# A graph kernel's gathered table: rows 1280 bytes apart in HBM and addressed by element, row slots 1056 bytes apart in SBUF

## What is computed

```
support = x @ W                      # x is normalised first
r_D = sigmoid(support @ a2)
gated = r_D * support
msg = gated[col] * edge_values[:, None]
out = segment_sum(msg, row, num_segments=n)
sumnorm = segment_sum(edge_values * r_D[col, 0], row, num_segments=n)
out = out / sumnorm[:, None]
```

## Time and profile before

| | us |
|---|---|
| median of 3 runs | 1783.61 |
| lowest, highest | 1783.45, 1788.98 |
| the profiled execution | 1787.5 |
| its span, first to last instruction | 1785.2 |
| GpSimd busy with the 599 gathers of L727 | 582.6 |
| GpSimd busy with the 294 gathers of L649 | 296.7 |
| TensorE busy, whole program | 1240.0 |
| VectorE busy, whole program | 1081.3 |

### The profile page before, as it was taken

One profiled execution on the slowest core, in us unless ns is written; L12 is line 12 of the kernel. 1 busy time (PEld: TensorE's weight loads), 2 busy tenths in 40 slices (PEclk: granted clock), 3 DMA queues, 4 the chain that ended last, 5 costly groups with the idle time before them and its releaser, 6 DMA issues.

```text
span 1785.2 us, 20679 instructions
## 1 busy us (share of the span) xinstructions
PE 1240.0 (69%) x5939; PEld 947.5 (53%) x5939; DVE 1081.3 (61%) x2748; ACT 361.8 (20%) x1172; POOL 945.3 (53%) x956
## 2 busy tenths in 40 slices
PE   5488666876776866565676767667676676768898
PEld 3377555755555655333454544445454454545787
DVE  8978896766787673344555555555555565556322
ACT  1255200000000000011222222222222222223233
POOL 0111176666666666566666666666666666664000
PEclk9699876878878778677787787877788787878999
DMA  7011143333333333733333333333333333332022
GB/s 221 8 58 59 35 76 92 94 90 94 101 87 93 95 88 99 110 99 94 91 94 92 100 97 90 100 90 101 91 99 98 91 100 91 99 94 60 28 71 73
DMA packets 120862, 158.14 MB, mean 89 GB/s; under 512 B 57903, under 2 KB 90307, under 8 KB 120764
## 3 DMA queue, kind: packets, MB, share of 16 engines
q0 software_dynamic: 44528, 119.20, 25.4%
q1 hardware_dynamic: 69180, 31.29, 6.9%
q10 hardware_dynamic: 7056, 6.45, 1.1%
HBM read 134.88 MB, written 21.98 MB: 88 GB/s over the span
## 4 chain that ended last, share of the span: by engine, by line
issue 38%; another core or an unknown queue 23%; PE 18%; DVE 9%; ACT 7%; DMA 2%; SPq 1%; DVEq 0%; POOLq 0%; ACTq 0%
PE bank L1499 17%; ACT big L1445 2%; DMA res<-in_x_dram 1%; ACT xT L1432 1%; DVE big L806 1%; ACT pos L1410 1%; DVE S L1131 1%; ACT xn L1423 1%; ACT lg L1436 1%; DVE neg L1169 1%; DVE ag L1142 1%; DMA srec<-sorted_edges_dram 1%; DVE big L846 1%; ACT bc L1405 0%
## 5 line engine op out<-in xcount | busy, mean ns | idle before, releaser
L727 POOL DMA_INDIRECT rows<-gated_rows_dram,ring_i x599 | 582.6, 973 | 324.6 <-issue 171.3
L1499 PE MATMUL bank<-rows,S 128*128 128x257 f32 (+1 forms) x2254 | 602.1, 412 | 66.3 <-issue 26.2
L1499 PEld LDWEIGHTS bank<-rows,S 128*128 128x128 f32 x2254 | 456.5, 210 | 205.0 <-issue 110.7
L649 POOL DMA_INDIRECT rows<-gated_rows_dram,lg x294 | 296.7, 1009 | 159.7 <-issue 82.9
L1499 PE MATMUL bank<-Wxs,xT 128*128 128x512 f32 x196 | 176.7, 1054 | 270.7 <-ACT xT L1432 270.6
L1499 PE MATMUL bank<-big 128*98 128x80 f32 (+2 forms) x1740 | 217.0, 284 | 145.3 <-issue 97.8
L1499 PEld LDWEIGHTS bank<-big 128*98 128x98 f32 (+1 forms) x1740 | 203.5, 201 | 165.8 <-issue 162.6
L1499 PEld LDWEIGHTS bank<-Wxs,xT 128*128 128x128 f32 x196 | 55.7, 314 | 333.7 <-ACT xT L1432 284.4
L1131 DVE TENSOR_SCALAR S<-iota,lof,srec 128x128 f32<-128x128 f32 x637 | 177.2, 358 | 3.5 <-PE bank L1499 3.1
L637 POOL DMA_INDIRECT sorted_edges_dram<-big,idx x52 | 64.9, 1248 | 202.8 <-ACT big L1318 94.3
L1194 DVE SCALAR_TENSOR_TENSOR bc<-bc 128x1 f32<-128x1 f32 x49 | 10.7, 219 | 246.5 <-ACT bc L1303 246.5
(11 more groups left out here) (226 smaller groups left out, 1326.3 us busy)
## 6 DMA issues: line engine op xcount, KB each, us to landing
rows<-gated_rows_dram,ring_i POOLq DMA_INDIRECT x599
gated_rows_dram<-rows SPq DMA_DIRECT2D x49, 128.5 KB, 2.7
overflow_sums_dram<-ovr ACTq DMA_DIRECT2D x49, 128.5 KB
ovr<-overflow_sums_dram SPq DMA_DIRECT2D x49, 128.5 KB
res<-in_x_dram SPq DMA_DIRECT2D x1, 6144.0 KB
out_dram<-S SPq DMA_DIRECT2D x48, 128.0 KB, 1.7
rows<-gated_rows_dram,lg POOLq DMA_INDIRECT x294
sorted_edges_dram<-big SPq DMA_DIRECT2D x2, 514.5 KB, 7.9
```

The source lines that it names most:

```text
L649: pool.indirect_dma_start(rows[:, turn(n), :], None, gtab[:, :], bass.IndirectOffsetOnAxis(ap=ring1[:, n:n + 1], axis=0)).then_inc(s_row[t ...
L727: pool.indirect_dma_start(rows[:, slot(b, u), :], None, gtab[:, :], bass.IndirectOffsetOnAxis(ap=ring_i[:, b // CH % 2, n:n + 1], axis=0)) ...
L1499: return nc.tensor.matmul(o, l, r, start=start, stop=stop, skip_group_check=True)
```

## The change

The table moves to the tensor that held the lists, and the lists move to the tensor that held the table. The table's rows are TW = 320 elements (1280 bytes) apart. The gather is given the whole tensor as a column of single elements, so its index is the source row's number times 320; `decode` makes that product with one more VectorE instruction. The 63 elements between two rows are set to zero by four new DMAs on SP's queue, which stand between the weights and x; GpSimd waits for them before the first gather. The row slots in SBUF are RSTEP = 264 elements (1056 bytes) apart. Lengths that named the lists (LL) are now LS. The branch for very uneven graphs, which this input does not take, is changed in the same way.

```
+TW = 320
+LL = NB * P * TW // 2
+RSTEP = 264
...
+        table = srt
+        table_rows = table.rearrange("(r w) o -> r (w o)", w=TW)
+        edges = gtab.rearrange("n (w o) -> (n w) o", o=1)
...
-        RW = max(SL * GW, 4736)
+        RW = max(SL * RSTEP, 4736)
...
-        rows = rows_t[:, 0:SL * GW].rearrange("p (u w) -> p u w", w=GW)
+        rows = rows_t[:, 0:SL * RSTEP].rearrange("p (u w) -> p u w", w=RSTEP)[:, :, 0:GW]
...
             for d, s in wloads:
                 sp.dma_start(d, s).then_inc(s_w, 16)
+            for lo in range(0, NB, 13):
+                n = min(13, NB - lo)
+                sp.dma_start(table_rows[lo * P:(lo + n) * P, GW:TW].rearrange("(b p) w -> p b w", p=P),
+                             zeros[:, 0:n * (TW - GW)].rearrange("p (b w) -> p b w", w=TW - GW)).then_inc(s_pad, 16)
             sp.dma_start(res[:, 0:LAST, :], x[0:LAST * P, :].rearrange("(b p) f -> p b f", p=P)).then_inc(s_x, 16)
...
-                sp.dma_start(gtab[ds(b * P, P), :], Gt[:, k, :]).then_inc(s_gd[k], 16)
+                sp.dma_start(table_rows[ds(b * P, P), 0:GW], Gt[:, k, :]).then_inc(s_gd[k], 16)
...
-                        rows[:, turn(n), :], None, gtab[:, :],
+                        rows[:, turn(n), :], None, table[:, :],
                         bass.IndirectOffsetOnAxis(ap=ring1[:, n:n + 1], axis=0)).then_inc(s_row[turn(n)], 16)
...
+            pool.wait_ge(s_pad, 16 * -(-NB // 13))
...
-            v.tensor_scalar(ring, r, 7, None, ALU.logical_shift_right).then_inc(s_idx, 1)
+            step(v.tensor_scalar(ring, r, 7, None, ALU.logical_shift_right))
+            v.tensor_scalar(ring, ring, TW, None, ALU.mult).then_inc(s_idx, 1)
```

More of the change, by code:

```diff
@@ L49 @@
 OFF = NB * PB1
-LL = OFF + NB * PB + OV * P + (EC - ECOL) * P
+LS = OFF + NB * PB + OV * P + (EC - ECOL) * P
 SL = 18
@@ L149, in build @@
         tmpi = carve(EC, I32)
-        zeros = carve(LL // P)
+        zeros = carve(LS // P)
         cnt, ntf, ctf, base = carve(NB), carve(NB), carve(NB), carve(NB)
@@ L307, in build @@
         s_const = sem("s_const")
+        s_pad = sem("s_pad")
         s_tick = sem("s_tick")
@@ L637, in send @@
                 pool.indirect_dma_start(
-                    srt[:, :], bass.IndirectOffsetOnAxis(ap=idx[:, k, h:h + 1], axis=0),
+                    edges[:, :], bass.IndirectOffsetOnAxis(ap=idx[:, k, h:h + 1], axis=0),
                     runs[k][:, h * RUN:(h + 1) * RUN], None).then_inc(s_run, 16)
@@ L682, in scatter @@
                         pool.sem_inc(s_tick, 1)
-                        pool.tensor_scalar(ring_s[:, k, :], ring_s[:, k, :], LL, None, ALU.add)
+                        pool.tensor_scalar(ring_s[:, k, :], ring_s[:, k, :], LS, None, ALU.add)
                     else:
@@ L713, in _ @@
                     pool.indirect_dma_start(
-                        orow, None, gtab[:, :], bass.IndirectOffsetOnAxis(ap=oidx, axis=0)).then_inc(s_orow, 16)
+                        orow, None, table[:, :], bass.IndirectOffsetOnAxis(ap=oidx, axis=0)).then_inc(s_orow, 16)
             pool.wait_ge(s_ovd, 1)
@@ L727, in tile @@
                     pool.indirect_dma_start(
-                        rows[:, slot(b, u), :], None, gtab[:, :],
+                        rows[:, slot(b, u), :], None, table[:, :],
                         bass.IndirectOffsetOnAxis(ap=ring_i[:, b // CH % 2, n:n + 1], axis=0)).then_inc(sem, 16)
@@ L773, in _ @@
             step(v.tensor_scalar(over[0:VB, :], iotap[0:VB, :], float(NB), None, ALU.is_ge))
-            step(v.scalar_tensor_tensor(firstc[0:VB, :], over[0:VB, :], float(LL - NB * PB1), firstc[0:VB, :], ALU.mult, ALU.add))
-            step(v.scalar_tensor_tensor(firstd[0:VB, :], over[0:VB, :], float(LL - NB * PB), firstd[0:VB, :], ALU.mult, ALU.add))
+            step(v.scalar_tensor_tensor(firstc[0:VB, :], over[0:VB, :], float(LS - NB * PB1), firstc[0:VB, :], ALU.mult, ALU.add))
+            step(v.scalar_tensor_tensor(firstd[0:VB, :], over[0:VB, :], float(LS - NB * PB), firstd[0:VB, :], ALU.mult, ALU.add))
             v.tensor_copy(idx[:, 0, 0:1], firstc[0:VB, :]).then_inc(s_idx0, 1)
@@ L1105, in _ @@
                     v.tensor_copy(oreci, orec[:, 0:1]).then_inc(s_oS, 1)
-                    dve.wait_ge(s_oS, t * 4 + 1)
-                    v.tensor_scalar(oidx, oreci, 7, None, ALU.logical_shift_right).then_inc(s_oidx, 1)
+                    dve.wait_ge(s_oS, t * 5 + 1)
+                    v.tensor_scalar(oidx, oreci, 7, None, ALU.logical_shift_right).then_inc(s_oS, 1)
+                    dve.wait_ge(s_oS, t * 5 + 2)
+                    v.tensor_scalar(oidx, oidx, TW, None, ALU.mult).then_inc(s_oidx, 1)
                     v.tensor_scalar(olo[:, 0:1], oreci, P - 1, None, ALU.bitwise_and).then_inc(s_oS, 1)
-                    dve.wait_ge(s_oS, t * 4 + 2)
+                    dve.wait_ge(s_oS, t * 5 + 3)
                     v.tensor_copy(olof, olo[:, 0:1]).then_inc(s_oS, 1)
-                    dve.wait_ge(s_oS, t * 4 + 3)
+                    dve.wait_ge(s_oS, t * 5 + 4)
                     v.tensor_scalar(oS, iota[:, :], olof, orec[:, 1:2], ALU.is_equal, ALU.mult).then_inc(s_oS, 1)
@@ L1658, in _ @@
                     pe.wait_ge(s_orow, t * 16 + 16)
-                    pe.wait_ge(s_oS, t * 4 + 4)
+                    pe.wait_ge(s_oS, t * 5 + 5)
                     pe.wait_ge(s_oadd, t + 1)
```

12 lines of the change are left out of this document (6 added, 6 removed).

## The result

The changed kernel took 1802.76 us (median; 1796.52 to 1804.84). The kernel before, measured beside it, took 1786.3 us. The ratio on record is 1.0078, with a 95% interval of 1.0049 to 1.0106 (the quotient of the two medians is 1.0092): slower by 9 to 19 us. The forecast was 1790.2, in a range from 1775 to 1806, with 0.59 on slower. So the direction was right and the time lies in the range, but 12.6 us over the point. The profiled execution is the quickest of the four (1796.52; span 1793.0 after 1785.2).

The account below looks back on a forecast made before the run. It took the DMA engines loading x to bound the opening and GpSimd's queue the gathering parts. Terms 8.0 + 0.6 + 0 - 2.0 = +6.6 us on the median of 1783.6 gave 1790.2 us, range 1775 to 1806.

Parts of the forecast that it names:

- The bound of the opening: Opening: the 16 DMA engines moving x set the limit; a later x delays VectorE's statistics and everything after equally.
- The pad stores: Opening, SP's queue ahead of x: four stores of 6272 runs add 8.0 us, range 5.8 to 11.6, all on the path.
- The higher bound of 29.7 ns: Opening: the price of one 252-byte run using the dearer fixed cost of 20.3 ns, giving 11.6 us for 392 runs.
- The index: Decodes on VectorE: one more product each, three of 15 before a waiting gather, adding 0.6 us.
- GpSimd's issue: Gathering parts: indexing by element adds 0 us to issuing a gather; the other end was 58 us.
- the dearer issue: Rival, gathering parts: 16 to 65 ns more per gather by element, 1804 to 1848 us; chance 0.10.
- The flight: Gathering parts: aligned rows and slots shorten a gather's transfer, given back at 63 GpSimd stops; gain 2 us.
- GpSimd's queue leads: Gathering parts: GpSimd's queue sets the pace, 1.25 us a gather and a stop of 3 us, 18.0 us a block.
- The rest: Table-row stores, moved lists, GpSimd's wait for the gap-filling stores, and TensorE's reads: no effect on time.
- Dear pads: Rival, opening: the gap-filling stores cost twice their bytes, 15.6 us in place of 8.0, 1798 us; chance 0.12.
- The stops: Rival, gathering parts: GpSimd's waits on the full slot ring, 181 us, vanish with alignment, about 1610 us; chance 0.04.
- the shorter flight: Rival, gathering parts: alignment halves a gather's payload time, saving 16 us over 63 stops, 1776 us; chance 0.10.

Follow-up runs that it names:

- the pads alone: The kernel before plus only the four pad stores ahead of x, into a tensor nothing reads, with GpSimd's wait for them: ratio 1.0052, 9.2 us.
- the pads of 64 columns: The changed kernel with gap-filling stores of columns 256 to 319 (256 bytes from 1024) in place of 63 columns, table stores waiting for them: ratio 1.0033, 5.9 us.
- element index alone: The changed kernel with rows and slots 257 elements apart, so no gap-filling stores and no alignment; gathers still indexed by single elements: ratio 1.0008.
- the table of run prices: Two versions of the kernel before, each with five separately waited store batches of 6272 runs ahead of x, 128 to 512 bytes: 14.7 to 45.7 ns a run.
- the half-row kernel: The changed kernel with each gather fetching only the first 128 of a row's 257 columns, slots filled with ones: ratio 1.0097 against the kernel before.
- wider table stores: The changed kernel without the gap-filling stores; the 49 table-row stores write all 1280 bytes of a row: ratio 0.9989 on one chip, 1.0025 on another.
- the changed kernel's second trace: The changed kernel run again unaltered: ratio 1.0067 against the kernel before, span 1800.1 us.

## Why the prediction was right or wrong

**The bound of the opening: right.** x's load is on the path without slack; what stood ahead of it moved the statistics and the first gather by 11 us, and the end by 9 to 14 (9.2 with the pads alone, 12.0 and 13.9 with the change).

**The pad stores, 8.0 us, bounds 5.8 to 11.6: the place right, the size too small.** They cost 11.0 (50.23 less 39.26), near the upper end. The term of the sum that was mis-sized is the price of a run, 22.0 ns, put together from loads: x's 1024-byte runs and the 24-byte runs of the lists. A run on 32-byte steps is cheaper than that (16.9 ns alone, 15 in place: 6.0 us / 392). These, which begin at 1028, cost 25.0 ns alone and 28 in place (11.0 us / 392). And I took 8.0 where my own price gave 8.6. The higher bound of 29.7 ns would have been the better choice, though for another reason than the one I had for it. My sentence that SP's four issues run in some 0.43 us each while the engines work off the weights was wrong as well: they took 8.55 us, though that time is not what they cost (above, the pads of 64 columns).

**The index, 0.6 us: not contradicted.** With the statistics 10.97 later, the first gather is 11.24 later. The 0.27 between them has the size of the first decode's product, but from the statistics to the first gather the traces of the kernels above with 18 slots take from 185.6 to 187.7 us, so it is not shown; the end time cannot show it either (element index alone: 1.0008, 0.9990 to 1.0026).

**GpSimd's issue, 0: right.** 946 ns by element and by row, and the dearer issue (0.10) did not come.

**The flight, a gain of 2 us: wrong, and so was the reading behind it.** The long part took 894.4 us after 894.1. From what the Trainium skill, "DMA: Bandwidth & Descriptors", section "How a descriptor splits into AXI transactions", states of beats I had estimated a tenth off each read. The gathers' packets of four rows in the long part took 240.0 ns in place of 244.6 by their mean, so 2%. Over the six traces with whole aligned rows the mean packet is 237.7 to 240.5 ns, over the six without 240.1 to 244.6: some 4 ns apart, where a tenth would be 24. But the larger error is that even a flight of 0.23 us less (half a row) is not given back at a stop. I had read a constant distance of 3.2 us between the last gather and the end of a stop as a cause. Shortening one of its parts showed that it is not. "GpSimd's queue leads" fell with it: 23 us taken off the queue moved nothing.

**The rest at nothing: right in the time.** One thing in it changed without effect: a table store lands in 1.7 us in place of 2.7 (2.2 with the element index alone, 1.8 with 1280 bytes).

```profile
sorted_edges_dram<-rows SPq DMA_DIRECT2D x49, 128.5 KB, 1.7
```

**The sum.** +6.6 was forecast; 12.0 (1.0067) to 13.9 us (1.0078) were measured. The pads' 3.0 and the flight's 2.0 account for 5.0 of the difference and leave 0.4 to 2.3 us, within the intervals. The point was put on a median of 1783.6, which with more runs is 1786.3: another 2.7 us of the 12.6 by which the point missed.

**The rivals.** Dear pads (0.12, 15.6 us, 1798) is nearest in time, with a size that is too large and, by the table of run prices, the wrong rule (below 512 bytes) for a right suspicion. The stops did not go, and the shorter flight was excluded by the half-row kernel.

## What to carry to other kernels

When a transfer is put ahead of the load that everything waits for, cost it by its runs and not by its bytes, and price the runs by where they begin and end: one column more (256 bytes from 1024 in place of 252 from 1028) nearly halved the price here, a place behind x made it too small to measure, and wider table stores made the pads needless. A distance that is constant in a trace is no cause until one of its parts has been changed; a kernel that shortens the suspected part, even if it leaves out half of the data, tells in one run. And when two traces differ by 8 us between two stages, look at a second trace of the same kernel first.

## What the runs showed of the hardware

Stores from SBUF to HBM in runs of 128 to 512 bytes cost 14.7 to 29.2 ns a run on each engine if both ends in HBM are on a multiple of 32 bytes, and 45.7 ns for 224 bytes with both ends off. With one end off they cost 3 to 6 ns more, but there the steps of the source in SBUF are off as well. For gathered reads of 1028 bytes, beginning on a multiple of 256 bytes took some 4 ns off a packet of 243 (237.7 to 240.5 ns in six traces, 240.1 to 244.6 in six).

A wait for TensorE can end much later than the record of TensorE's work. The trace holds the moments at which the count of finished matmuls (`s_seg`) went up. In the kernel before, the matmul that ends the stop near 1017 us is recorded at 1009.80, and the count went up at 1016.98. In the first part four matmuls are recorded at 409.66, 412.51, 414.64 and 418.13, and their four counts came at 419.76, 419.81, 419.85 and 419.89, closer together than matmuls can follow each other by their records (0.43 us from one tile to the next). So counts are held back and come in a bunch, and the stops end with such a late count. What holds them back is open. I had thought of GpSimd's gathers: such waits often end when GpSimd has paused, 2.1 us after the last gather of the part in the kernel before and 4.3 in the changed kernel's second trace. But in the kernel with the pads behind x the same wait ("remote") ended at 713.67, between gathers at 712.45 and 713.70 that follow each other without a pause. So a pause is not needed.

The same kernel ran 0.9% quicker on one chip (1770.4 after 1786.4). In the traces of four kernels there the long part took 885 us in place of 894, at the same gather medians and the same granted clock (0.80 in 800 to 1600 us, on both).
